# Graph network of four layers on one core: node tables moved with four neighbouring rows per partition

## The chip, the cores and the metric

One core of a Trainium2 chip runs the whole kernel as one launch; the other cores are idle. The metric is the device time of one execution in microseconds, as the median over runs. The kernel before took 3378.82 us (median of 3 runs, 3373.29 to 3382.97).

## The reference, cut to what matters

There are 10,000 nodes with 512 float32 features and 5,000 edges sorted by destination. Each of four layers takes `h = relu(layernorm(x))`, computes something per edge from the source rows of `h`, sums it over the edges of each destination, and adds a node term:

```
h = maximum(layernorm(x), 0)
x = x + L0(h)   # MLP on [h[src], edge_attr], mean over dst, MLP on [h, mean]
x = x + L1(h)   # 8-head attention over edges, sum over dst, + h, layernorm
x = x + L2(h)   # degree-normalised convolution, self loops, relu
x = x + L3(h)   # project to 128, weight, sum over dst, project back to 512
```

About 4 of 10 nodes have an incoming edge; the others get zero for the sum over edges.

## The kernel before, in words

The program runs ten stages one after the other (`program`, L2507). All engines meet between two stages. Each tile in on-chip memory carries the letter of its stage:

- `a` (`prepare`, L138): loads and splits weights, and builds from `src` and `dst` the out-degree of every node, whether it has an incoming edge, and its slot (the row of the edge table that holds its sum). The counts come from one-hot matrices and matrix products: `hl` holds for every edge the partition of its node and the tile of its node.
- `b`, `d`, `f`, `h` (edge stages): gather rows of the node table by `src`, work on 128 edges at a time and write one row of sums per edge to an edge table T in HBM. `s` and `e` are the softmax and the sums of layer 1.
- `c`, `n`, `g`, `i` (node stages, L724, L1499, L1858, L2425): go over the nodes in order. A group is 512 nodes (4 tiles of 128), 20 groups in all. For each group they load the dense rows of the node table from HBM (1 MB), gather the sums from T with four indirect DMAs (one per tile, by `slot`; a node without an edge has an index out of bounds, and its row isn't fetched), compute, and store the dense rows of the next node table (1 MB).

The node tables between stages (`x1`, `x2`, `x3`) are in HBM with one node per row and 10,240 rows; `x2` has 516 columns (2,064 bytes a row), the others 512 (2,048 bytes). Input and output have 10,000 rows. The edge stages gather from these tables by node number.

`group_rows` (L43) is the view through which dense loads and stores see a table: tile j of a group holds rows 128 j to 128 j + 127 of it, one per partition, so each partition takes four rows that lie 256 KB apart. The degree, presence and slot tables (`dis`, `dis2`, `dish`, `has`, `slot`) are [128 partitions x 80 tiles] and follow the same order.

The dense transfers are issued by SyncE in all four node stages, and the final stores by ScalarE's queue; the gathers by GpSimd. In stage `i` the work of a group is: SyncE waits until the store of two groups ago has landed in HBM (L2448), then loads `X` (L2449); ScalarE fills `G` with a constant (L2469), GpSimd gathers over it (L2463); VectorE waits for both and adds them (L2499); ScalarE's queue stores the result (L2477). There are two buffers (b = 0, 1), so the second group runs beside the first. The last group has only 272 nodes, and is loaded and stored tile by tile: 128, 128 and 16 rows (L766, L2482).

Of the kernel before, what the change touches and what calls it, by code (L numbers as in the profile page):

```python
# [6 lines left out]
I32 = mybir.dt.int32  # L7
U32 = mybir.dt.uint32
U16 = mybir.dt.uint16
ALU = mybir.AluOpType  # L10
ACT = mybir.ActivationFunctionType

P = 128
NODES = 10000
# [12 lines left out]
GROUP = 4  # L27
NEW = P - 1
ET = 40
# [3 lines left out]
NG = NT // GROUP  # L33
NR = NG // 2
# [2 lines left out]
EPS = 1e-5  # L37
XW = F + 4
FAR = 1.0e6
assert ET * NEW >= EDGES and NT * P >= NODES and (ET - 1) * NEW < EDGES  # L40


def group_rows(table, g, cols):  # L43

    return table[bass.ds(g * (GROUP * P), GROUP * P), 0:cols].rearrange("(j p) f -> p j f", p=P)


def tiles(x, width=F):
# [37 lines left out]
class Core:  # L86
# [18 lines left out]
    def sb(self, stack, name, shape, dt=F32):  # L105
        return stack.enter_context(self.nc.sbuf_tensor(name, shape, dt))
# [31 lines left out]
def prepare(nc, core, a, keep, l0):  # L138
# [14 lines left out]
    with ExitStack() as st:  # L153
        sb = lambda n, s, d=F32: core.sb(st, "a_" + n, s, d)
        dst_i, nxt_i, src_i, typ_i = (sb(n, [P, ET], I32) for n in ("dst", "nxt", "src", "typ"))
        wgt = sb("wgt", [P, ET])
        emb = sb("emb", [P, HEADS * HEADS])
        hl = sb("hl", [P, 4, ET], I32)
        last = sb("last", [P, ET])
        val = sb("val", [P, ET])  # L160
        iota_i = sb("iotai", [P, P], I32)
# [32 lines left out]
        with nc.Block() as block:  # L194
# [76 lines left out]
            def _(dve):  # L271
                n = 0

                def step(ins):
                    nonlocal n
                    n += 1
                    ins.then_inc(dve_step, 1)
                    dve.wait_ge(dve_step, n)
# [7 lines left out]
                dve.wait_ge(idx_loaded, 16 * 6)  # L286
                step(dve.tensor_copy(iota_f[:, :], iota_i[:, :]))
                for k, ids in enumerate((src_i, dst_i)):
                    step(dve.tensor_scalar(hl[:, 2 * k, :], ids[:, :], 127, None, ALU.bitwise_and))
                    step(dve.tensor_scalar(hl[:, 2 * k + 1, :], ids[:, :], 7, None, ALU.logical_shift_right))  # L290

                step(dve.tensor_tensor(last[:, :], dst_i[:, :], nxt_i[:, :], ALU.not_equal))
                step(dve.tensor_tensor(val[:, :], last[:, :], slot_i[:, :], ALU.mult))
# [430 lines left out]
def layer0_nodes(nc, core, a, keep, T0, x1):  # L724
# [3 lines left out]
    x_loaded = [sem("c_x0"), sem("c_x1")]  # L728
# [7 lines left out]
    stored = [sem("c_st0"), sem("c_st1")]  # L736
# [3 lines left out]
    with ExitStack() as st:  # L740
        sb = lambda n, s, d=F32: core.sb(st, "c_" + n, s, d)
        X = sb("X", [P, 2, GROUP, F])
# [17 lines left out]
        with nc.Block() as block:  # L760
            @block.sync
            def _(sp):
                def load(g, b):
                    sp.dma_start(X[:, b, :, :], group_rows(a["x"], g, F)).then_inc(x_loaded[b], 16)

                def load_last(buf, b, sems):  # L766

                    at = (NG - 1) * GROUP * P
                    left = NODES - at
                    for j in range((left + P - 1) // P):  # L770
                        n = min(P, left - j * P)
                        sp.dma_start(buf[0:n, b, j, :], a["x"][at + j * P:at + j * P + n, :]).then_inc(sems[b], 16)

                def residual(g, b):
                    sp.dma_start(XB[:, b, :, :], group_rows(a["x"], g, F)).then_inc(res_loaded[b], 16)

                def store(r, g, b):
                    sp.wait_ge(o_out, r * GT + (4 * b + 4 + 2))
                    sp.dma_start(group_rows(x1, g, F), XB[:, b, :, :]).then_inc(stored[b], 16)

                for b in range(2):
                    load(b, b)
                sp.dma_start(W3raw, a["L0_gnn_W3"][0:F, :].rearrange("(k p) n -> p k n", p=P)).then_inc(w3_loaded, 16)
                sp.dma_start(W4raw, a["L0_gnn_W4"].rearrange("(k p) n -> p k n", p=P)).then_inc(w_loaded, 16)
                sp.dma_start(b3[:, :], a["L0_gnn_b3"].rearrange("(k p) -> p k", p=P),
                             allow_slow_non_contiguous=True).then_inc(w_loaded, 16)
                sp.dma_start(b4[:, :], a["L0_gnn_b4"].rearrange("(o n) -> o n", o=1).broadcast_to([P, F])).then_inc(w_loaded, 16)
                sp.wait_ge(init, 2)
                with sp.Fori(0, NR - 2) as r:
                    sp.wait_ge(tp_ready, r * TPR + 2 * KF)  # L790
                    for b in range(2):
                        load(r * 2 + (2 + b), b)
                    for b in range(2):
                        sp.wait_ge(stored[b], r * 16)
                        residual(r * 2 + b, b)
                    for b in range(2):
                        store(r, r * 2 + b, b)
                for r in (NR - 2, NR - 1):
                    sp.wait_ge(tp_ready, r * TPR + 2 * KF)
                    for b in range(2):  # L800
                        if r == NR - 1:
                            load(b, b)
                        elif b:
                            load_last(X, b, x_loaded)
                        else:
                            load(2 * r + 2, b)
                    for b in range(2):
                        sp.wait_ge(stored[b], 16 * r)
                        if r == NR - 1 and b:
                            load_last(XB, b, res_loaded)  # L810
                        else:
                            residual(2 * r + b, b)
                    for b in range(2):
                        store(r, 2 * r + b, b)
                for b in range(2):
                    sp.wait_ge(stored[b], 16 * NR)
                    sp.wait_ge(x_loaded[b], 16 * (NR + 1) + 32 * b)

            @block.gpsimd
            def _(pool):  # L820
                pool.memset(G[:, :, :, :], 0.0).then_inc(init, 1)
                pool.memset(XB[:, 1, :, :], 0.0).then_inc(init, 1)
                pool.wait_ge(w_loaded, 48)
                pool.wait_ge(init, 2)

                def round_(r, late):
                    pool.tensor_copy(idx[:, :], keep["slot"][:, bass.ds(r * GT, GT)]).then_inc(idx_staged, 1)
                    pool.wait_ge(idx_staged, r + 1)
                    pool.wait_ge(u_out, r * (2 * GT) + 4)
                    pool.sem_inc(go, 1)  # L830
                    for i in range(GT):
                        pool.indirect_dma_start(G[:, i // GROUP, i % GROUP, :], None, T0[:, :],
                                                bass.IndirectOffsetOnAxis(idx[:, i:i + 1], 0),
                                                bounds_check=ROWS_E - 1, oob_is_err=False).then_inc(run_loaded[i // GROUP], 16)
                    for b in range(2):
                        pool.wait_ge(res_loaded[b], r * 16 + (16 + late * b))
                        pool.tensor_tensor(XB[:, b, :, :], XB[:, b, :, :], over(b4[:, :].unsqueeze(1), [P, GROUP, F]),  # L837
                                           ALU.add).then_inc(res_ready, 1)
                    for b in range(2):
                        pool.wait_ge(run_loaded[b], r * 64 + 64)  # L840
                    pool.sem_inc(go, 1)

                with pool.Fori(0, NR - 1) as r:
                    round_(r, 0)
                round_(NR - 1, 32)

            @block.scalar
            def _(act):
# [41 lines left out]
            def _(dve):  # L890
# [70 lines left out]
                with dve.Fori(0, NR - 2) as r:  # L961
                    round_(r, 0)
                for r in (NR - 2, NR - 1):
                    round_(r, 32)

            @block.tensor
            def _(pe):
# [1457 lines left out]
def layer3_nodes(nc, core, a, keep, x3, T3, out):  # L2425
# [4 lines left out]
    x_loaded, run_loaded, stored = ([sem(f"i_{n}{b}") for b in range(2)] for n in ("x", "g", "st"))  # L2430
    out_ready = sem("i_out")
    with ExitStack() as st:
        sb = lambda n, s, d=F32: core.sb(st, "i_" + n, s, d)
        X = sb("X", [P, 2, GROUP, F])
# [5 lines left out]
        with nc.Block() as block:  # L2440
# [25 lines left out]
            @block.scalar  # L2466
            def _(act):
                def fill(b):
                    act.copy(G[:, b, :, :], over(const[:, :].unsqueeze(1), [P, GROUP, F])).then_inc(filled, 1)  # L2469

                act.wait_ge(const_out, 1)
                fill(0)
                fill(1)
                with act.Fori(0, NR - 1) as r:
                    for b in range(2):
                        act.wait_ge(out_ready, r * 2 + (b + 1))
                        act.dma_start(group_rows(out, r * 2 + b, F), X[:, b, :, :]).then_inc(stored[b], 16)  # L2477
                        fill(b)
                act.wait_ge(out_ready, NG - 1)
                act.dma_start(group_rows(out, NG - 2, F), X[:, 0, :, :]).then_inc(stored[0], 16)  # L2480
                act.wait_ge(out_ready, NG)
                at = (NG - 1) * GROUP * P  # L2482
                for j in range((NODES - at + P - 1) // P):
                    n = min(P, NODES - at - j * P)
                    act.dma_start(out[at + j * P:at + j * P + n, :], X[0:n, 1, j, :]).then_inc(stored[1], 16)
                act.wait_ge(stored[0], 16 * NR)
                act.wait_ge(stored[1], 16 * (NR - 1) + 48)

            @block.vector
            def _(dve):  # L2490
# [124 lines left out]
```

## Time and profile before

| | |
|---|---|
| median of 3 runs | 3378.82 us |
| span of the profiled execution | 3386.8 us |
| busy: TensorE, weight loads, VectorE, ScalarE, GpSimd | 71%, 61%, 53%, 36%, 30% |
| DMA packets | 189,198, 354.10 MB |
| of them SyncE's queue | 129,536, 239.71 MB |
| GpSimd's gathers | 42,880, 91.15 MB |
| ScalarE's queue | 16,688, 21.99 MB |

The span is the time from the first to the last instruction of one profiled execution on the core. It is 8.0 us over the median of the timed runs; no separate device time of this execution is listed. "DMA share" in the rows is the mean busy share of the 16 DMA engines of the core. A DMA is cut into packets; the rows give their number, their bytes and the time they took, as a share of the time of 16 engines. Queue q1 is SyncE's, q10 ScalarE's, q0 GpSimd's.

### The profile page before, as it was taken

Reading aid. Unit: us, or ns where it says so; the run is one execution under the profiler, and the core shown is the slowest. Engines: PE = TensorE matmul, PEld = TensorE weight load, DVE = VectorE, ACT = ScalarE, POOL = GpSimd, SP = SyncE. Lnnn points to the kernel's source line nnn. Section 1 sums busy time; section 2 is a strip of 40 time slices with the busy share of each in tenths; the row PEclk is TensorE's granted clock in tenths of the full one; section 3 lists DMA queues with packets and bytes.
Section 4 is the critical chain, followed back from the end, with each engine's and each line's share of the span. In section 5 each row is a group of like instructions: output and inputs, shape, how many; then the busy total and the mean of one; then the engine's idle time right before and its main releaser. Section 6 shows DMA issues by size and latency. Waiting matters only on the chain. (4 is left out here: it accounts for less than half of the span.)

```text
span 3386.8 us, 41659 instructions
## 1 busy us (share of the span) xinstructions
PE 2409.5 (71%) x13104; PEld 2063.8 (61%) x13104; DVE 1788.8 (53%) x3382; ACT 1223.3 (36%) x2110; POOL 1006.1 (30%) x839
## 2 busy tenths in 40 slices
PE   6779999999969999999979849200005969966600
PEld 6779888888859888888867736100003557754400
DVE  4523232323334544455446565699974579955522
ACT  2133233333333333233335533333324545534421
POOL 0000000000012332233133313566553067752065
PEclk9889999999979999999979965555555589988855
DMA  5101101010224232422243302343434255543388
GB/s 173 37 14 49 37 32 41 27 41 23 41 90 140 87 100 98 140 95 91 81 137 88 85 15 84 121 152 126 139 114 145 82 175 178 179 148 113 112 286 269
DMA packets 189198, 354.10 MB, mean 105 GB/s; under 512 B 28605, under 2 KB 41917, under 8 KB 189097
## 3 DMA queue, kind: packets, MB, share of 16 engines
q1 hardware_dynamic: 129536, 239.71, 20.4%
q0 software_dynamic: 42880, 91.15, 9.7%
q10 hardware_dynamic: 16688, 21.99, 1.9%
q8 instruction: 61, 1.00, 0.1%
q14 instruction: 33, 0.26, 0.0%
HBM read 279.42 MB, written 128.16 MB: 120 GB/s over the span
## 5 line engine op out<-in xcount | busy, mean ns | idle before, releaser
L1848 PE MATMUL f_s_ps<-f_Yh,f_match 128*128 128x258 f32 x80 | 40.1, 501 | 415.3 <-issue 414.7
L1848 PEld LDWEIGHTS f_s_ps<-f_Yh,f_match 128*128 128x128 f32 x80 | 24.7, 309 | 442.0 <-issue 438.0
L132 PE MATMUL b_y_ps<-W23h,b_Rh 128*128 128x320 f32 x800 | 249.1, 311 | 0.0
L470 POOL DMA_INDIRECT b_X<-in_x,b_idx x48 | 48.4, 1008 | 669.3 <-PE b_tp_ps L659 655.4
L133 PE MATMUL b_y_ps<-W23l,b_Rh 128*128 128x320 f32 x800 | 246.2, 308 | 0.5 <-issue 0.5
L134 PE MATMUL b_y_ps<-W23h,b_Rl 128*128 128x320 f32 x800 | 246.1, 308 | 0.3
L132 PE MATMUL b_hid_ps<-b_hTh,W1h 128*128 128x512 f32 x500 | 202.9, 406 | 13.2 <-issue 13.2
L132 PE MATMUL c_u_ps<-c_W3h,c_hTh 128*128 128x320 f32 x640 | 202.0, 316 | 0.0
L133 PE MATMUL b_hid_ps<-b_hTl,W1h 128*128 128x512 f32 x500 | 201.4, 403 | 0.0
L134 PE MATMUL b_hid_ps<-b_hTh,W1l 128*128 128x512 f32 x500 | 201.1, 402 | 0.0
L591 DVE TENSOR_TENSOR b_Rl<-b_R,b_Rh 128x512 fp32r<-128x512 f32 x100 | 69.3, 693 | 248.6 <-ACT b_Rh L524 248.6
L134 PE MATMUL c_u_ps<-c_W3h,c_hTl 128*128 128x320 f32 x640 | 198.4, 310 | 0.0
L133 PE MATMUL c_u_ps<-c_W3l,c_hTh 128*128 128x320 f32 x640 | 198.3, 310 | 0.0
L837 POOL TENSOR_TENSOR c_XB<-c_XB,c_b 128x2048 f32<-128x2048 f32 x20 | 91.6, 4598 | 345.1 <-DMA c_XB<-in_x 345.1
L869 ACT ACTIVATE c_R<-c_tp_ps,c_b 128x512 f32<-128x512 f32 x100 | 68.8, 688 | 323.1 <-PE c_tp_ps L971 314.9
L132 PE MATMUL c_o_ps<-c_W4h,c_zh 128*128 128x512 f32 x400 | 161.8, 405 | 6.4 <-DVE c_zl L917 6.1
L134 PE MATMUL c_o_ps<-c_W4h,c_zl 128*128 128x512 f32 x400 | 156.5, 391 | 0.0
L133 PE MATMUL c_o_ps<-c_W4l,c_zh 128*128 128x512 f32 x400 | 156.1, 390 | 0.0
L616 DVE TENSOR_TENSOR b_Yl<-b_y_ps,b_Yh 128x320 fp32r<-128x320 f32 x80 | 39.4, 492 | 219.9 <-ACT b_Yh L536 219.9
L133 PEld LDWEIGHTS b_y_ps<-W23l,b_Rh 128*128 128x128 f32 x800 | 150.1, 188 | 1.5 <-issue 1.1
L132 PEld LDWEIGHTS b_y_ps<-W23h,b_Rh 128*128 128x128 f32 x800 | 150.0, 188 | 1.1 <-issue 0.7
L134 PEld LDWEIGHTS b_y_ps<-W23h,b_Rl 128*128 128x128 f32 x800 | 149.9, 187 | 0.0
(326 smaller groups left out, 7505.5 us busy)
## 6 DMA issues: line engine op xcount, KB each, us to landing
c_X<-in_x SPq DMA_DIRECT2D x21, 1024.0 KB
x<-n_O SPq DMA_DIRECT2D x20, 1032.0 KB, 4.7
g_X<-x SPq DMA_DIRECT2D x20, 1032.0 KB
x<-c_XB SPq DMA_DIRECT2D x20, 1024.0 KB, 4.7
n_X<-x SPq DMA_DIRECT2D x20, 1024.0 KB, 8.9
x<-g_O SPq DMA_DIRECT2D x20, 1024.0 KB
i_X<-x SPq DMA_DIRECT2D x20, 1024.0 KB
c_XB<-in_x SPq DMA_DIRECT2D x19, 1024.0 KB
```

Source lines behind the costliest of these rows:

```text
L132: pe.matmul(out, ah, bh, start=first, stop=False)
L133: pe.matmul(out, ah, bl, start=False, stop=False)
L134: return pe.matmul(out, al, bh, start=False, stop=last)
L470: pool.indirect_dma_start(X[:, i // GROUP, i % GROUP, :], None, a["x"][:, :], bass.IndirectOffsetOnAxis(idx[:, i:i + 1], 0), bounds_check= ...
L591: dve.tensor_tensor(Rl[:, m, :], R[:, :], Rh[:, m, :].bitcast(F32), ALU.subtract).then_inc(hid_lo, 1)
L616: dve.tensor_tensor(Yl[:, t % 2, w], y[:, h, 0:HALF], Yh[:, t % 2, w].bitcast(F32), ALU.subtract).then_inc(y_out[h], 1)
L837: pool.tensor_tensor(XB[:, b, :, :], XB[:, b, :, :], over(b4[:, :].unsqueeze(1), [P, GROUP, F]), ALU.add).then_inc(res_ready, 1)
L869: act.activation(R[:, k % 2, :], tp[:, k % 2, :], ACT.Relu, bias=b3[:, c:c + 1]).then_inc(z_hi, 1)
L1848: pe.matmul(s[:, 2 * j + h, 0:HW], match[:, b, j, :], Yh[:, j, w], start=True, stop=False)
```

## The change

`group_rows` is turned: partition p holds rows 4 p to 4 p + 3 of the group, so that a partition's four rows are neighbours in HBM. A partition's share of a group is then 8,192 bytes in one piece (8,256 in `x2`) on both sides. The tables follow: a node's partition is bits 2 to 8 of its number, and its tile is four times the bits from 9 up plus the lowest two. The last group covers 68 partitions with all four rows each, moved as 64 and 4 partitions (`LAST`). The edge stages and the tables in HBM stay as they are.

```
+LAST = ((0, 64), (64, 4))
 def group_rows(table, g, cols):
-    return table[bass.ds(g * (GROUP * P), GROUP * P), 0:cols].rearrange("(j p) f -> p j f", p=P)
+    return table[bass.ds(g * (GROUP * P), GROUP * P), 0:cols].rearrange("(p j) f -> p j f", p=P)
@@ prepare: VectorE, for src and dst each
-  step(dve.tensor_scalar(hl[:, 2 * k, :], ids[:, :], 127, None, ALU.bitwise_and))
-  step(dve.tensor_scalar(hl[:, 2 * k + 1, :], ids[:, :], 7, None, ALU.logical_shift_right))
+  step(dve.tensor_scalar(hl[:, 2 * k, :], ids[:, :], 2, 127, ALU.logical_shift_right, ALU.bitwise_and))
+  step(dve.tensor_scalar(within[:, :], ids[:, :], GROUP - 1, None, ALU.bitwise_and))
+  step(dve.tensor_scalar(hl[:, 2 * k + 1, :], ids[:, :], 9, 2, ALU.logical_shift_right, ALU.logical_shift_left))
+  step(dve.tensor_tensor(hl[:, 2 * k + 1, :], hl[:, 2 * k + 1, :], within[:, :], ALU.add))
@@ stage c, SyncE (and the waits on these semaphores: 16 per DMA, so 16 where 32 was)
 def load_last(buf, b, sems):
-    at = (NG - 1) * GROUP * P
-    left = NODES - at
-    for j in range((left + P - 1) // P):
-        n = min(P, left - j * P)
-        sp.dma_start(buf[0:n, b, j, :], a["x"][at + j * P:at + j * P + n, :]).then_inc(sems[b], 16)
+    for p, n in LAST:
+        at = (NG - 1) * GROUP * P + p * GROUP
+        sp.dma_start(buf[p:p + n, b, :, :], a["x"][at:at + n * GROUP, :].rearrange("(p j) f -> p j f", p=n)
+                     ).then_inc(sems[b], 16)
@@ stage i, ScalarE's queue: the store of the last group
-  for j in range((NODES - at + P - 1) // P):
-      n = min(P, NODES - at - j * P)
-      act.dma_start(out[at + j * P:at + j * P + n, :], X[0:n, 1, j, :]).then_inc(stored[1], 16)
+  for p, n in LAST:
+      at = (NG - 1) * GROUP * P + p * GROUP
+      act.dma_start(out[at:at + n * GROUP, :].rearrange("(p j) f -> p j f", p=n), X[p:p + n, 1, :, :]).then_inc(stored[1], 16)
```

## Rows read from the trace of the kernel before

**Rows 1.** Busy time by stretch: stages c, n, g, i (us, engines, clock, DMA, GB/s).

```profile
core 0: us, PE busy (x) PEld busy (x) DVE busy (x) ACT busy (x) POOL busy (x), PEclk, DMA share, GB/s
987.00:1700.00 713.00, 654.41 (x3872) 587.18 (x3872) 356.67 (x628) 239.40 (x389) 186.13 (x115) 0.97 0.32 108
2145.00:2528.00 383.00, 0.00 (x0) 0.00 (x0) 338.74 (x611) 121.22 (x181) 234.62 (x111) 0.50 0.40 133
2707.00:3019.00 312.00, 261.48 (x1280) 213.40 (x1280) 255.08 (x501) 154.19 (x261) 200.16 (x181) 0.94 0.50 166
3196.00:3387.00 191.00, 2.07 (x2) 0.50 (x2) 46.78 (x22) 37.87 (x20) 107.94 (x100) 0.50 0.79 262
```

**Rows 2.** Waits in stage i, 3195 to 3387: us in total, times, longest.

```profile
DVE i_X L2499 <- DMA i_G<-T,i_idx: 93.8, 15, 9.6
DVE i_X L2499 <- DMA i_X<-x: 37.6, 5, 8.9
...
SPq L2449 <- DMA out<-i_X: 146.3, 16, 22.8
```

**Rows 3.** Chain that ended last, one turn of stage i: start, us, what.

```profile
3269.76 8.63 DMA out<-i_X
...
3278.55 8.14 DMA i_X<-x
```

**Rows 4.** DMA from 327.2 to 331 us: one 256 KB load, one 320 KB store.

```profile
DMA packets 288, 0.59 MB, mean 155 GB/s; under 512 B 32, under 2 KB 32, under 8 KB 288
```

**Rows 5.** DMA from 3204 to 3206 us: only node rows, 2,048-byte packets.

```profile
DMA packets 411, 0.81 MB, mean 406 GB/s; under 512 B 15, under 2 KB 15, under 8 KB 411
q1 hardware_dynamic: 411, 0.81, 106.1%
```

**Rows 6.** DMA from 41 to 43 us: only a weight, 5,120-byte packets.

```profile
q1 hardware_dynamic: 163, 0.83, 102.6%
```

**Rows 7.** DMA queues from 3208 to 3387 us: packets, MB, share of 16 engines.

```profile
q1 hardware_dynamic: 9504, 18.88, 33.8%
q10 hardware_dynamic: 10352, 20.48, 31.5%
q0 software_dynamic: 6400, 8.10, 14.2%
```

**Rows 8.** Waits for loads, gathers and stores in stages c, n, g.

```profile
DVE n_G L1641 <- DMA n_G<-T,n_idx: 20.7, 5, 6.6
...
DVE n_raw L1620 <- DMA n_X<-x: 14.9, 1, 14.9
...
DVE c_raw L897 <- DMA c_X<-in_x: 9.5, 2, 9.3
...
SPq L1925 <- DMA x<-g_O: 3.9, 1, 3.9
```

**Rows 9.** Start of the kernel, VectorE: start, us, instruction, idle before.

```profile
11.66 0.18 DVE L289 TENSOR_SCALAR a_hl<-a_src 128x40 int32<-128x40 int32 x1
...
14.80 0.83 DVE L282 CAST rows<-a_rows 128x1280 uint16<-128x1280 int32 x1 [1.83 <-DMA a_rows<-in_dst_row]
```

**Rows 10.** End of the kernel: last add and the three last stores.

```profile
3380.57 2.29 DVE L2499 TENSOR_TENSOR i_X<-i_X,i_G 128x2048 f32<-128x2048 f32 x1 [1.14 <-DMA i_G<-T,i_idx]
3382.90 1.35 ACTq L2485 DMA_DIRECT2D out<-i_X  x3
```

**Rows 11.** Stage n: the last gather of a round and who waited for it.

```profile
2303.54 1.21 POOL L1565 DMA_INDIRECT n_G<-T,n_idx  x1 [0.30 <-issue]
...
2310.26 5.65 DVE L1641 SCALAR_TENSOR_TENSOR n_G<-n_G,has,n_H 128x512 f32<-128x512 f32 x2 [6.38 <-DMA n_G<-T,n_idx]
```

**Rows 12.** DMA queues from 2305.5 to 2308.5 us, the whole list.

```profile
q1 hardware_dynamic: 404, 0.83, 98.0%
```

**Rows 13.** Stage i, gathers and fills: busy us, mean ns | idle.

```profile
L2463 POOL DMA_INDIRECT i_G<-T,i_idx x80 | 99.9, 1248 | 72.3 <-ACT i_G L2469 51.3 <-issue 16.4 <-POOL i_idx L2458 2.7
...
L2469 ACT COPY i_G<-i_const 128x2048 f32<-128x2048 f32 x20 | 37.9, 1898 | 145.2 <-DVE i_X L2499 127.4 <-DVE i_const L2494 17.8
```

More of the change, by code:

```diff
@@ L39 @@
 FAR = 1.0e6
+LAST = ((0, 64), (64, 4))
+assert (NG - 1) * GROUP * P + sum(n for _, n in LAST) * GROUP == NODES and len(LAST) == 2
 assert ET * NEW >= EDGES and NT * P >= NODES and (ET - 1) * NEW < EDGES
 def group_rows(table, g, cols):
-    return table[bass.ds(g * (GROUP * P), GROUP * P), 0:cols].rearrange("(j p) f -> p j f", p=P)
+    return table[bass.ds(g * (GROUP * P), GROUP * P), 0:cols].rearrange("(p j) f -> p j f", p=P)
 def tiles(x, width=F):
@@ L158, in prepare @@
         hl = sb("hl", [P, 4, ET], I32)
+        within = sb("within", [P, ET], I32)
         last = sb("last", [P, ET])
@@ L816, in _ @@
                     sp.wait_ge(stored[b], 16 * NR)
-                    sp.wait_ge(x_loaded[b], 16 * (NR + 1) + 32 * b)
+                    sp.wait_ge(x_loaded[b], 16 * (NR + 1) + 16 * b)
             @block.gpsimd
@@ L844, in _ @@
                     round_(r, 0)
-                round_(NR - 1, 32)
+                round_(NR - 1, 16)
             @block.scalar
@@ L963, in _ @@
                 for r in (NR - 2, NR - 1):
-                    round_(r, 32)
+                    round_(r, 16)
             @block.tensor
@@ L2481, in _ @@
                 act.wait_ge(out_ready, NG)
-                at = (NG - 1) * GROUP * P
-                for j in range((NODES - at + P - 1) // P):
-                    n = min(P, NODES - at - j * P)
-                    act.dma_start(out[at + j * P:at + j * P + n, :], X[0:n, 1, j, :]).then_inc(stored[1], 16)
+                for p, n in LAST:
+                    at = (NG - 1) * GROUP * P + p * GROUP
+                    act.dma_start(out[at:at + n * GROUP, :].rearrange("(p j) f -> p j f", p=n), X[p:p + n, 1, :, :]).then_inc(stored[1], 16)
                 act.wait_ge(stored[0], 16 * NR)
-                act.wait_ge(stored[1], 16 * (NR - 1) + 48)
+                act.wait_ge(stored[1], 16 * (NR - 1) + 32)
             @block.vector
```

## The prediction

> **What bounds the kernel now.** I read the busy time by stage first [rows 1]. In stage c TensorE works 92% of the time and the DMA engines 32%; stage g is TensorE, VectorE and GpSimd with DMA at 50%; stage n is VectorE (339 of 383 us). Only the last stage, i, is bound by transfers: VectorE works 47 of 191 us and the DMA engines are busy 79% of the time. Next I read who waits there [rows 2]: VectorE's adds wait 93.8 us for the gathers (15 times of 20) and 37.6 us for the dense load (5 times), and SyncE waits 146.3 us for stores to land before it may load into the same buffer. The chain of waits shows the loop [rows 3]: a store of 1 MB takes 8.6 us from its issue to its landing, the load that follows it 8.1 us. With the add (2.3 us [rows 10]) and the issues this is a turn of some 19 us for two groups. So a change in what 1 MB costs the DMA engines is felt in stage i, and at the other node stages only where they start, end, or wait for a gather.
>
> **Does the change make larger packets at all?** It does if four neighbouring rows become one packet. The edge attributes are loaded in just such a shape, [128 partitions, 4, 128] contiguous on both sides. In that stretch there are 288 packets: 128 of 2,560 bytes and 16 small ones of the store, which leaves 144 for the 256 KB load, that is 128 pieces of 2,048 bytes and 16 small ones [rows 4]. Unmerged there would be 512 pieces. So I expect 128 packets of 8,192 bytes for each MB where there are 512 now.
>
> **What a packet costs.** Undisturbed, 396 packets of 2,048 bytes (411 less the 15 small) took 106.1% of 16 engines in 2 us: 33.95 us / 396 = 85.7 ns [rows 5]. Packets of 5,120 bytes took 102.6% x 32 us / 163 = 201.4 ns [rows 6]. The line through both is 8.6 ns a packet plus 0.0377 ns a byte, so 8,192 bytes would take 317 ns against 4 x 85.7 = 343 now. A MB is 8 such packets on each engine: 8 x 26 ns = 0.21 us less, of some 2.7. The bounds are 0 (both rates are near one ceiling, 406 and 0.83 MB / 2 us = 415 GB/s) and what follows.
>
> In stage i packets cost more than that: SyncE's take 33.8% x 179 us x 16 / 9,216 = 105 ns (18 loads of 512), ScalarE's 31.5% x 2,864 us / 10,000 = 90 ns [rows 7]. Over the undisturbed 85.7 this is 9,216 x 19.3 / 16 + 10,000 x 4.5 / 16 = 11.1 + 2.8 = 13.9 us per engine. If this excess is paid per packet, three quarters of it go (10.4 us); if per byte, nothing. No row says which. I take a fifth of that, 2 us, since packets two and a half times larger show none of it changing beyond the line, and keep 0 and 10.4 for the range.
>
> On small pieces the Trainium skill (DMA: Bandwidth & Descriptors, Why small descriptors are slow) gives about 3 cycles of fixed overhead a packet, at the 850 MHz of its fabric 3.5 ns; my fit of this trace has 8.6. By that page the saving would be, as an estimate, 24 packets x 3.5 ns = 0.08 us a MB, and the last stage would gain about 3 us instead of 8. The measured line decides here.
>
> **The sum, part by part.**
> Stage i: 39 dense MB (20 loads, 19 full stores) x 0.21 = 8.2 us, plus 2 for the excess. Adds wait for gathers more often than for loads, but a gather itself lands only after the dense transfer ahead of it has drained: the last gather of a round in stage n was issued at 2303.5 and waited for until 2310.3, and for three of those microseconds the list of queues shows SyncE's alone, at 98% [rows 11, 12]. So dense transfers are in both chains. The engines are busy 79% of the stage; that share of 10.2 us is -8.1 us. If the dense time were never what ends last, it would be 0.
> Starts: VectorE waits for the first 1 and 2 MB in c and n [rows 8], and g opens like c: 4 x 0.21 = -0.8. Ends: SyncE waits 3.9 us for a last store in each of c, n and g (one row stands for three): -0.6.
> Stage n waits 20.7 us for gathers in 5 rounds of 10 [rows 8]; with the longest at 6.6 that is about three full waits, each behind two dense MB: 3 x 2 x 0.21 = -1.3, of which I take half, -0.6, bounds 0 and -1.3. Other dense transfers of c, n and g are loaded ahead and hidden by TensorE or VectorE; if this cover were gone, they would gain too, not lose.
> Stage a: four more small VectorE steps (0.18 us, 0.22 with the gap: 0.9 us). The conversion behind them waits 1.83 us for its own load [rows 9], so they are hidden: 0; uncovered, +0.9.
> Last group: in c two loads and residuals lose one issue on SyncE's queue, none of which is waited for: 0. At the end of i, three stores at 1.35 us of issue become two [rows 10]: -0.45. The one that carries the data now has 64 partitions. No row shows a 64-partition store; the three stores and their landing take 3.9 us from issue to the end (3382.9 to 3386.8), so I bound the effect by -0.5 and +1.2 (its 0.5 MB at half of 415 GB/s is 2.5 us against 1.3) and take +0.4, together 0.
> The Trainium skill (SBUF, State Buffer, Door 1: The DMA port swizzle) speaks against this one: partitions 0 to 63 reach only half of the 16 ports. By it the last store would run at half rate, an estimate of 1.2 us more; no trace here shows it.
>
> Sum: -8.1 - 0.8 - 0.6 - 0.6 = -10.1 us. The profiled span would go from 3386.8 to 3376.7; it is 8.0 us over the median, so the median goes from 3378.8 to 3368.7. I forecast **3369 us**.
>
> **The rivals.**
> A. The excess goes with the packets, and all of it is exposed: stage i gains (8.2 + 10.4) x 0.79 to x 1.0 = 15 to 19 us, with the 2 us elsewhere 17 to 21: 3358 to 3362, 3360 in the middle. For it: loads cost 105 ns a packet beside stores and 86 alone. Against: what disturbs them may be the memory, which sees the same bytes.
> B. The gain is hidden. GpSimd spends 4 x 1.25 us on a group's gathers, and add, fill and gather form a loop of their own (2.3 + 0.5 + 1.9 + 5.0 us and the landing of some 4) [rows 13]. If that loop sets the pace, only starts and ends are left, -1 to -3: 3376 to 3378. Against: a turn is 19 us now, this loop some 14.
> C. The other side: the gathers are held back longer. A gather is in small pieces: 6,400 packets in 80 gathers, 5 for each engine [rows 7]. If a piece must let one dense packet pass, it waits 317 ns where it waited 86: 5 x 0.23 = 1.2 us for a gather that shares the engines. The last gather of a group decides in 15 of 20 adds [rows 2]: +18 us, and +3 to +6 in n's rounds, against the -10.1 above: +11 to +14, 3390 to 3393. It decides from about 0.55 us a gather on, in more than half of the groups. For it: 15 of 20. Against: in rows 12 the queues don't take turns; the gather waits for the whole transfer, and that gets shorter. The Trainium skill (DMA: Bandwidth & Descriptors, Queues, rings and completion order) has the engines go round the queues packet by packet, which would make C the rule.
> D. The view isn't merged, or merged only on one side: 512 packets stay, 3378 to 3380. Against: rows 4.
>
> **How the numbers follow.** Forecast (own range -5 to -15, 3364 to 3374): 0.50. A: 0.17. B and D: 0.20 (0.17 and 0.03). C: 0.13, of which a third ends near zero. A difference of 0.3% is 10.1 us, about what this kernel's runs tell from nothing (they spread by 9.7 us). My forecast stands on that line, so half of its chance is on either side: faster 0.25 + 0.17 = 0.42; same 0.25 + 0.20 + 0.04 = 0.49; slower 0.09. The range reaches from A's far end with the spread of the runs, 3352, to the middle of C, 3386.
>
> **What would show it.** Right: SyncE's packets fall from 129,536 by 160 x 384 = 61,400 (c moves 60 full MB on it, n and g 40 each, i 20) and ScalarE's by 7,300; 8 KB packets at some 317 ns; stage i shorter by 6 to 10 us and no other stage by more than 2; store and load of the chain nearer 8.2 and 7.8 us. A: stage i shorter by over 14. B: the turn unchanged with adds waiting for gathers 20 of 20. C: waits for gathers in i and n longer than 93.8 and 20.7 us. The prediction is wrong if stage i gets longer, or if a stage that I call covered moves by over 3 us.

## The result, and the profile after

The changed kernel takes 3351.52 us (median of 5 runs, 3344.72 to 3364.01) against 3378.82 before (5 runs, 3373.29 to 3383.71). The medians are 27 us apart; the ratio of the runs is 0.9929, 95% interval 0.9907 to 0.9952, or 24 us. I had forecast 3369, a gain of 10. The direction is right and the size is not: the gain is 2.4 to 2.7 times the forecast, and the time lies half a microsecond below the low end of my range (3352).

The profiled span went from 3386.8 to 3358.2 us. By stage, in us from the first instruction of one to the first of the next (b is 828.1 and 826.3, s and e together 184.5 and 184.3):

| | a | c | d | n | f | g | h | i |
|---|---|---|---|---|---|---|---|---|
| before | 159.4 | 711.6 | 261.4 | 383.2 | 179.4 | 312.3 | 176.5 | 190.4 |
| after | 160.2 | 689.9 | 258.7 | 386.8 | 179.0 | 310.5 | 176.2 | 186.3 |

Stage c, which I had called covered, gave 21.7 us; stage i, on which the forecast stood, gave 4.1 instead of 8.1. The windows of c and i of the kernel after answer to [rows 1]: VectorE's busy time in c fell by 13.3 us with the same 628 instructions, so some of them had been slower before.

```profile
core 0: us, PE busy (x) PEld busy (x) DVE busy (x) ACT busy (x) POOL busy (x), PEclk, DMA share, GB/s
986.50:1676.40 689.90, 652.33 (x3872) 586.95 (x3872) 343.38 (x628) 239.61 (x389) 188.15 (x113) 0.97 0.30 112
...
3171.90:3358.20 186.30, 2.08 (x2) 0.50 (x2) 46.77 (x22) 37.89 (x20) 111.23 (x100) 0.50 0.76 269
```

**The packets.** The page after lists SyncE's queue (q1) with 61,904 packets fewer than before for the same bytes, and ScalarE's (q10) with 7,528 fewer:

```profile
q1 hardware_dynamic: 67632, 239.71, 19.2%
q0 software_dynamic: 42880, 91.15, 9.7%
q10 hardware_dynamic: 9160, 21.99, 1.8%
```

What an 8 KB packet costs undisturbed stands in the list of queues of the kernel after from 2127 to 2132 us, the answer to [rows 5]. Less 32 small ones there are 259 in q1's line: 100.4% x 5 us x 16 / 259 = 310 ns, against 343 for four of 2 KB and my 317.

```profile
DMA packets 296, 2.13 MB, mean 426 GB/s; under 512 B 32, under 2 KB 32, under 8 KB 37
...
q1 hardware_dynamic: 291, 2.12, 100.4%
```

**Stage i.** The queues from 3185 to 3358 us (173 us; before, [rows 7], it was 179):

```profile
q1 hardware_dynamic: 2592, 18.88, 32.2%
q10 hardware_dynamic: 2824, 20.48, 29.8%
q0 software_dynamic: 6334, 8.02, 15.1%
```

A full packet of q1 takes 32.2% x 173 x 16 / 2,304 = 387 ns where four took 420. That is 77 ns over the undisturbed 310; before it was 420 - 343 = 77 as well. ScalarE's stores went from 361 to 330 ns per 8 KB, 18 and 20 ns over. In this stage none of the excess went with the packets. The two queues together are busy for 62.0% x 173 = 107.3 us where it was 65.3% x 179 = 116.9: 9.6 us less, against 10.2 in my sum.

The waits of stage i after, to set beside [rows 2], show that loads hardly end last any more:

```profile
DVE i_X L2502 <- DMA i_G<-T,i_idx: 118.9, 18, 9.6
DVE i_X L2502 <- DMA i_X<-x: 7.7, 2, 4.2
```

Gathers and loads together held the adds for 131.4 us before (93.8 and 37.6) and 126.6 now. The chain of waits, which went through a store and a load at [rows 3], now goes mostly through the add, ScalarE's fill and the gather; here is one of its turns, in the columns of [rows 3]:

```profile
3318.49 1.91 ACT i_G L2473
...
3323.88 2.22 POOL i_G L2467
3326.40 6.63 DMA i_G<-T,i_idx
3333.12 2.30 DVE i_X L2502
```

**The end.** The last add and the last stores after (compare [rows 10]), and the queue of those stores from 3350 to 3358.2 us. From the first issue to the end it is 3352.5 to 3358.2 = 5.7 us, where it was 3.9; I had forecast no difference.

```profile
3350.14 2.29 DVE L2502 TENSOR_TENSOR i_X<-i_X,i_G 128x2048 f32<-128x2048 f32 x1 [8.26 <-DMA i_G<-T,i_idx]
3352.47 1.31 ACTq L2488 DMA_DIRECT2D out<-i_X  x2
```

```profile
q10 hardware_dynamic: 88, 0.56, 32.2%
```

32.2% x 8.2 us x 16 / 68 full packets is 621 ns each, twice the undisturbed 310. The last stores of the kernel before, mostly from 128 partitions, stand in its list of queues from 3382.9 to 3386.8 us. Less 64 small ones there are 316 packets of 2 KB at 94 ns, or 377 ns per 8 KB:

```profile
q10 hardware_dynamic: 380, 0.65, 47.7%
```

The Trainium skill (SBUF, State Buffer, Door 1: The DMA port swizzle) has partitions 0 to 63 reach half of the ports. The trace agrees in part: 8 KB on each of 16 engines in 621 ns is 211 GB/s, half of the 423 of undisturbed loads, but the last stores before ran at 348 only.

**Stage c, where the gain is.** The rows of VectorE's operation `c_zl = c_R - c_zh`, first before, then after (busy us, mean ns of one | idle):

```profile
L917 DVE TENSOR_TENSOR c_zl<-c_R,c_zh 128x512 fp32r<-128x512 f32 x100 | 100.2, 1025 | 63.5 <-ACT c_zh L870 35.9 <-issue 16.7 <-ACT c_R L869 10.8
```

```profile
L921 DVE TENSOR_TENSOR c_zl<-c_R,c_zh 128x512 fp32r<-128x512 f32 x100 | 86.6, 889 | 55.0 <-ACT c_zh L874 29.1 <-ACT c_R L873 13.8 <-issue 12.1
```

The list of `c_zl` gives 676 ns as its shortest and 4,806 as its longest before, and 677 and 3,764 after. One round of c (two groups) shows what holds it. In the rows of before, GpSimd adds the bias to the residual once that has landed, and a `c_zl` that starts inside these 9.13 us ends only with them:

```profile
1085.10 1.80 SPq L764 DMA_DIRECT2D c_X<-in_x  x2
...
1098.72 9.13 POOL L837 TENSOR_TENSOR c_XB<-c_XB,c_b 128x2048 f32<-128x2048 f32 x2 [36.62 <-DMA c_XB<-in_x]
...
1103.60 5.41 DVE L917 TENSOR_TENSOR c_zl<-c_R,c_zh 128x512 fp32r<-128x512 f32 x2 [0.64 <-ACT c_zh L870]
```

The same three rows after:

```profile
1083.23 1.68 SPq L769 DMA_DIRECT2D c_X<-in_x  x2
...
1094.78 9.20 POOL L841 TENSOR_TENSOR c_XB<-c_XB,c_b 128x2048 f32<-128x2048 f32 x2 [33.93 <-DMA c_XB<-in_x]
...
1101.77 3.37 DVE L921 TENSOR_TENSOR c_zl<-c_R,c_zh 128x512 fp32r<-128x512 f32 x2 [0.63 <-ACT c_zh L874]
```

From the first load's issue to the add it was 13.6 us and is 11.6: the residual lands 2.1 us earlier. So the adds begin 7.0 us ahead of VectorE instead of 4.9, and what is left of them when `c_zl` comes is 2.2 us instead of 4.2. The two operations (1.4 us alone) took 5.4 and take 3.4.

The other rounds are alike: in each of the ten, before and after, one `c_zl` meets the adds and ends 0.55 us behind them. Its time fell by 1.6 to 2.0 us in the first eight rounds and not at all in the last two. Together this is the 13.6 us of the two rows above. TensorE's transposes wait for the split. These are the waits of PE for `c_zl`, before:

```profile
PE c_tp_ps L971: 21.5, 20
PE c_o_ps L132: 6.1, 5
```

And after, 18.6 us less, near the stage's 21.7:

```profile
PE c_tp_ps L975: 7.6, 12
PE c_o_ps L134: 1.4, 2
```

That is the theory that the experiments test: **larger packets let the residual land earlier, and GpSimd's add gets out of the way of VectorE's split.** Why 2.1 us, when my line gives 5 MB x 0.21 = 1.0? The queue list of the 20 us from the first of these loads on (before: 1085 to 1105, after: 1083.2 to 1103.2) has

```profile
GB/s 352 389 389 332 242 176 156 184 319 356 348 373 410 336 393 418 381 397 402 406 406 393 385 385 385 389 389 385 389 180 29 12 0 0 0 0 0 0 0 0
DMA packets 2640, 5.24 MB, mean 262 GB/s; under 512 B 80, under 2 KB 80, under 8 KB 2640
...
q1 hardware_dynamic: 2640, 5.24, 75.4%
```

before and

```profile
GB/s 360 508 295 508 131 131 377 410 442 393 426 442 377 475 442 360 459 410 426 459 393 459 459 360 442 328 49 0 0 0 0 0 0 0 0 0 0 0 0 0
DMA packets 710, 5.16 MB, mean 258 GB/s; under 512 B 80, under 2 KB 80, under 8 KB 80
...
q1 hardware_dynamic: 710, 5.16, 64.5%
```

after. Less 80 small packets, 8 KB cost 4 x 75.4% x 320 us / 2,560 = 377 ns before and 64.5% x 320 / 630 = 328 after, 49 ns less instead of 26. A slow stretch behind the store is part of it: four half microseconds at 156 to 242 GB/s before, two at 131 after. Here, unlike in stage i, half of the excess (34 to 18 ns) went with the packets. 5 MB x 8 packets x 49 ns is 2.0 us, which is the 2.1.

### The profile page after: what moved, and what is told of

It is laid out like the page before. It is cut to its first block and busy times, and to the rows that moved or that the text cites. A ratio compares the mean times of both kernels' runs of the same rounds, so it can differ in the third digit from the quotient of the medians.

```text
span 3358.2 us, 41660 instructions
## 1 busy us (share of the span) xinstructions
PE 2403.5 (72%) x13104; PEld 2060.3 (61%) x13104; DVE 1775.6 (53%) x3386; ACT 1224.0 (36%) x2110; POOL 1001.8 (30%) x839
## 5 line engine op out<-in xcount | busy, mean ns | idle before, releaser
L475 POOL DMA_INDIRECT b_X<-in_x,b_idx x48 | 48.4, 1008 | 668.1 <-PE b_tp_ps L664 654.2
```

The source lines that it names most:

```text
L475: pool.indirect_dma_start(X[:, i // GROUP, i % GROUP, :], None, a["x"][:, :], bass.IndirectOffsetOnAxis(idx[:, i:i + 1], 0), bounds_check= ...
```

## The experiments

Each is compared with the kernel before on its own chip. Stage times are from one profile each, in us, by the starts of the stages as above; `c_zl` is its mean in ns.

| kernel | ratio to before, 95% interval | c | `c_zl` | n | i |
|---|---|---|---|---|---|
| after | 0.9929 [0.9907, 0.9952] | 689.9 | 889 | 386.8 | 186.3 |
| e1_small_packets | 0.9972 [0.9952, 0.9993] | 702.2 | 1010 | 376.5 | 195.6 |
| e11_small_packets_again | 0.9984 [0.9969, 0.9999] | 702.7 | 1006 | 376.8 | 192.9 |
| e2_small_in_c | 0.9951 [0.9926, 0.9976] | 700.9 | 1008 | 372.7 | 187.0 |
| e3_before_residual_first | 0.9954 [0.9934, 0.9974] | 693.0 | 691 | 367.5 | 189.2 |
| e4_after_residual_first | 0.9937 [0.9912, 0.9962] | 690.4 | 691 | 378.4 | 188.4 |
| e5_before_no_add | 0.9939 [0.9923, 0.9954] | 680.6 | 690 | 375.9 | 190.0 |
| e6_after_no_add | 0.9888 [0.9872, 0.9903] | 679.8 | 690 | 371.7 | 185.2 |
| e9_after_again | 0.9897 [0.9883, 0.9911] | 685.8 | 896 | 371.6 | 180.9 |
| e10_before_again | 0.9998 [0.9988, 1.0009] | 702.7 | 1012 | 377.1 | 189.1 |
| e12_after_adds_in_pieces | 0.9898 [0.9870, 0.9925] | 683.7 | 801 | 373.1 | 184.4 |
| e13_before_adds_in_pieces | 0.9905 [0.9879, 0.9932] | 686.6 | 892 | 372.0 | 192.4 |
| e14_after_pieces_residual_first | 0.9941 [0.9916, 0.9967] | 690.4 | 690 | 382.6 | 188.0 |

e5, e6, e9 and e10 ran on another chip, where the kernel before takes 3302 us; stages d, f and h are shorter there for both kernels, so only ratios and the stages c, n and i are compared across chips.

**Packets of 2 KB in the new order.** Four spare elements behind each row keep the tile from being one piece; e1 has it in c, n, g and i, e2 in c alone, e11 is e1 again.

```
-X = sb("X", [P, 2, GROUP, F])
+X = sb("X", [P, 2, GROUP, F + 4])[:, :, :, 0:F]
```

> The changed kernel, with the tiles of all dense loads and stores given a row pitch of 4 elements more, so that a partition's four rows are neighbours in HBM but not on chip: the order of rows and all tables stay as changed, and each MB is cut into 512 packets of 2 KB again. Theory 1 (the gain comes from larger packets): the gain is gone, 3374 to 3384 us, stage c back from 690 to about 712 us, the packets of SyncE's queue back at about 129,500. Theory 2 (the gain comes from the order in which the memory is walked, four neighbouring rows per partition): the gain stays, 3347 to 3360 us, stage c about 690 us.

> The changed kernel with the wider row pitch in stage c alone (X and the residual tile), so 2 KB packets there and 8 KB packets in n, g and i. Theory 1 (most of the gain lies in stage c, where the residual lands earlier and GpSimd's add of the bias meets VectorE's split of the hidden rows for a shorter time): stage c about 712 us, the split of zl at about 1,025 ns mean, the whole 20 to 23 us slower than the changed kernel, 3370 to 3376 us. Theory 2 (stage c's 22 us are a matter of this one execution, and the gain lies in n, g, i): within 4 us of the changed kernel, 3348 to 3358 us.

> The changed kernel with its new row order, but with four spare elements behind each 512-element row of the X and XB tiles of stage c, the X and O tiles of stages n and g and the X tile of stage i, so that the merged transfers move in 2,048-byte packets. Theory packet size (the gain comes from fewer, larger packets, by way of earlier landings): the ratio to the kernel before is about 1.000 (0.997 to 1.002), stage c takes about 702 us and stage i 189 to 190 us. Rival row order (neighbouring rows per partition help whatever the packet size): ratio 0.990 to 0.995, stage c 686 to 690 us.

With the small packets stage c is back at 700.9 to 702.7 us and `c_zl` at 1,006 to 1,010 ns: the new row order doesn't do it, the packets do, and e2 shows it with the packets of c alone (the 11 us are of its profile; its ratio stands only 7 us from that of the changed kernel, where I expected 20 to 23). Stage i goes to 195.6 and 192.9. What e1 and e11 keep of the gain, 0.16% to 0.28%, is 5 to 9 us that neither theory had; whether it is the row order, the wider pitch or scatter was not settled.

**The residual loaded ahead of the activations**, so that the add is over before VectorE's split begins.

```
+for b in range(2):                     # stored[b], then residual(2 * r + b, b) or load_last
+    ...
 sp.wait_ge(tp_ready, r * TPR + 2 * KF)
 for b in range(2):
     load(r * 2 + (2 + b), b)
 ...
-for b in range(2):                     # the residual, from behind the loads
-    ...
```

> The kernel before with one thing moved: in stage c SyncE issues the two residual loads of a round ahead of the two loads of the next rows, not behind them. Packets stay at 2 KB. Collision theory: the residual lands about 5 us earlier, GpSimd's adds end before VectorE's split begins, the split falls from a mean of 1,025 ns to about 690 to 750 ns, stage c from 712 to 680 to 690 us, the whole 3347 to 3360 us: as much as the change gains or more, without any larger packet. Rival (larger packets help TensorE's stage in some other way, for example by less traffic beside its reads): stage c stays within 4 us of 712.

> The changed kernel with the same move: residual loads ahead of the loads of the next rows. Collision theory: what is left of the collision goes too (the split's mean of about 890 ns to 690 to 750), stage c from 690 to 678 to 686 us, the whole 3338 to 3348 us, faster than both kernels; and between this kernel and the one before with the same move only stages n, g, i and the ends are left, 3 to 8 us. Rival: the rows now come later, and VectorE's statistics wait for them: stage c 5 us or more longer than 690.

In e3 the split is at its undisturbed 691 ns with packets of 2 KB, and stage c loses 10 to 19 us to the two profiles of before (702.7 and 711.6). One round of e3, to set beside the rows of before: the add runs from 1096.4 to 1105.7, and the first split begins behind it.

```profile
1096.44 9.24 POOL L837 TENSOR_TENSOR c_XB<-c_XB,c_b 128x2048 f32<-128x2048 f32 x2 [29.52 <-DMA c_XB<-in_x]
...
1108.02 0.69 DVE L917 TENSOR_TENSOR c_zl<-c_R,c_zh 128x512 fp32r<-128x512 f32 x1 [0.63 <-ACT c_zh L870]
```

With this collision gone for both, the packets are worth 2.6 us in c (693.0 and 690.4), not 20. But both stages are longer than expected (680 to 690 and 678 to 686), and e4 gains nothing on the changed kernel (0.9937 and 0.9929), though its `c_zl` is 200 ns shorter a piece. The reason stands at the start of the stage. The first adds now run while VectorE splits the weights W4 (`c_W4l`), again with two operands in on-chip memory, and that is held instead. The row of the kernel after, then two of e4:

```profile
1019.75 2.83 DVE L128 TENSOR_TENSOR c_W4l<-c_U,c_W4h 128x2560 fp32r<-128x2560 f32 x1 [1.54 <-ACT c_W4h L123]
```

```profile
1015.16 9.14 POOL L841 TENSOR_TENSOR c_XB<-c_XB,c_b 128x2048 f32<-128x2048 f32 x2
...
1017.03 9.96 DVE L128 TENSOR_TENSOR c_W4l<-c_U,c_W4h 128x2560 fp32r<-128x2560 f32 x1 [1.53 <-ACT c_W4h L123]
```

So 7.1 us are lost once, and the first `c_zl` comes 58.9 us after the start of the stage instead of 50.5. The time from the first `c_zl` of a round to that of the next is 64.6 us in e4 and 65.3 in the kernel after, so the later rounds win back most of it. VectorE waits no longer for the activations than before the move (8.3 us against 8.6), so the rival that I had named isn't the reason.

**No add**, in c only: four columns in place of 512. The output of this layer then lacks the bias in the other 508 columns.

```
-pool.tensor_tensor(XB[:, b, :, :], XB[:, b, :, :], over(b4[:, :].unsqueeze(1), [P, GROUP, F]),
+pool.tensor_tensor(XB[:, b, :, 0:4], XB[:, b, :, 0:4], over(b4[:, 0:4].unsqueeze(1), [P, GROUP, 4]),
```

> The kernel before with the collision taken away where it starts: in stage c GpSimd adds the bias b4 to 4 columns of the residual only, not to all 512, so the other 508 columns of the layer's output lack b4 (left out). Loads, waits and packets stay. Collision theory: without the two adds of 4.6 us a round, VectorE's split of zl takes 690 ns each time, stage c goes from 712 to 685 to 695 us. Rival (early transfers help the stage by themselves): stage c stays above 702 us.

> The changed kernel with the same part left out (b4 is added to 4 of 512 columns). Collision theory: it has nothing more to gain in stage c, 685 to 692 us, within 3 us of the kernel before without the add: the size of the packets then makes no difference to this stage. Rival (larger packets help stage c beyond the collision): 8 us or more shorter in stage c than the kernel before without the add.

> The changed kernel, unedited, once more, to have its stages a second time and its time beside the same runs of the kernel before as the experiments. If the stage times of the first look are the kernel's own: c 687 to 693 us, i 185 to 188, n 367 to 387 (this stage has moved by 19 us between executions whatever the packets), the ratio to before 0.991 to 0.995. If stage c's 690 us was chance: c over 698.

> The kernel before, unedited, for a second profile. If its stage c is its own: 708 to 715 us with the split of zl at a mean of 1,000 to 1,040 ns. If the residual's arrival moves the collision from execution to execution: c anywhere from 695 to 712, and the 22 us of the first pair of profiles overstate the change; the stage's mean gain is then 10 to 15 us.

This is the sharpest test. Both stages are even shorter than expected. Without GpSimd's add stage c takes 680.6 us with 2 KB packets and 679.8 with 8 KB ones. So of the 16.9 us that the same two kernels differ by in c on this chip with the add (702.7 and 685.8), 16 need the add. The second profiles also show that the first pair's 21.7 us in c overstates the change by some microseconds: the kernel before has 711.6 in one and 702.7 in the other, on another chip. Stage i of e9, 180.9 us, is outside the 185 to 188 expected. e9 and e10 repeat the result there: 0.9897 against 0.9998, a gain of 33 us (from 3302) with c 16.9, i 8.2 and n 5.5 of it. e5 and e6 still differ by 0.51%, 17 us, of which their profiles show 12.4 (3271.0 and 3258.6), 0.8 in c.

**The adds of c and n in four pieces**, meant to leave gaps in which VectorE gets its turn; in e14 with the residual first as well.

```
+for j in range(GROUP):
+    add = pool.tensor_tensor(XB[:, b, j, :], XB[:, b, j, :], b4[:, :], ALU.add)
+add.then_inc(res_ready, 1)
```

> The changed kernel, with GpSimd's bias adds of stage c and stage n made as four instructions of 128x512 in place of one of 128x2048. Theory collision (VectorE's operations on two SBUF operands stand still while one long GpSimd add runs): no such VectorE operation is held for more than about a quarter of 4.6 us, stage c takes 680 to 685 us and stage n 345 to 365 us, the whole 20 to 30 us less than the changed kernel. Rival (the two engines share the port element by element, or the lock is for the sum of the adds): stage c stays at 684 to 690 us, stage n at 370 to 387 us.

> The kernel before with the same adds in pieces. Theory collision: most of what the change gains in stage c is the escape from the collision, so stage c is within 3 us of the changed kernel's with pieces, and the two kernels with pieces differ by 8 to 12 us, what stage i and the ends are worth. Rival: the difference stays at 27 to 36 us.

> The changed kernel with adds in pieces and with the residual of stage c loaded ahead of the activations. Theory collision: with pieces the place of the add no longer matters, so it is within 3 us of the kernel with pieces alone. Rival (the order still matters, since an add in front of the splits never meets them and one behind does): stage c shorter by 5 us or more than with pieces alone, or longer by as much if the activations' later landing costs more.

No `c_zl` takes over 1,782 ns now. In e13 this alone (in c and n), with the old packets, gives c 686.6 us and a ratio of 0.9905: about as much as the whole change. GpSimd's adds in c end later for it (109.4 us of work instead of 91.6), so it isn't their end or what GpSimd does behind them that made the stage long, but what they hold up. Stage c differs from e12's by 2.9 us, as the theory wanted. The totals of e12 and e13 are 0.9898 and 0.9905, 2 us apart where I expected 8 to 12; the intervals are each about 9 us to either side, so this neither confirms nor refutes it, and their profiles have i 8.0 us apart. Stage n was a miss: 373 us, not 345 to 365. The operation on `n_G`, which the long add had held, is quicker, and the time comes back as waiting for gathers. Stage n of the kernel after, and of e12:

```profile
L1645 DVE SCALAR_TENSOR_TENSOR n_G<-n_G,has,n_H 128x512 f32<-128x512 f32 x80 | 133.3, 1676 | 27.8 <-DMA n_G<-T,n_idx 24.2 <-ACT n_H L85 3.7
```

```profile
L1647 DVE SCALAR_TENSOR_TENSOR n_G<-n_G,has,n_H 128x512 f32<-128x512 f32 x80 | 84.5, 1066 | 59.4 <-DMA n_G<-T,n_idx 59.4
```

48.8 us less busy, 31.6 more idle, and GpSimd's own adds cost 125.2 us in pieces against 96.3. e14 is no better than e12, and its profile has c 6.7 us longer, so the order still matters. It is `c_W4l` again, and here the pieces don't help: it comes in the third of eight pieces and ends 2.7 us behind the last, after 9.46 us.

```profile
1016.63 9.98 POOL L842 TENSOR_TENSOR c_XB<-c_XB,c_b 128x512 f32<-128x512 f32 x8
...
1019.84 9.46 DVE L128 TENSOR_TENSOR c_W4l<-c_U,c_W4h 128x2560 fp32r<-128x2560 f32 x1 [1.54 <-ACT c_W4h L123]
```

Why `c_zl` gets in between two pieces and `c_W4l` doesn't is open. The best time is e12's, 3341.63 us, 10 us less than the changed kernel by the ratios where I expected 20 to 30, but its interval overlaps that of the changed kernel, so it is shown to be faster only than the kernel before.

## Why the prediction was right or wrong

**Larger packets: right.** 61,904 and 7,528 packets fewer, against 61,400 and 7,300. Rival D is out.

**The cost of a packet: nearly right.** 310 ns undisturbed, against 317: 33 ns less than four small ones instead of 26.

**The excess of stage i: too high.** I gave a fifth of it to the packets; none went (77 ns per 8 KB before and after). The two errors cancel: 9.6 us of DMA time, against 10.2. Rival A, whose extra came from this excess, is nearest in its total (3358 to 3362), but by accident: it wanted stage i over 14 us shorter.

**Stage i, -8.1: not settled.** It got 4.1 us shorter in the first pair of profiles and 8.2 in the second. The profiles with 8 KB packets in i (after, e2, e4, e6, e9, e12, e14) have it at 185.7 us on average (180.9 to 188.4), those of the old order (before, e3, e5, e10, e13) at 190.2, and the new order with 2 KB (e1, e11) at 194.3. By these means the packets are worth 8.5 us, near my term, and everything else that changed costs 4.0, of which 1.8 is the last store. With such a spread that is an indication only, and the padded pitch of e1 and e11 may be part of it, in which case the packets are worth less. Rival B, that the loop of add, fill and gather takes over, is half true: gathers end 18 of 20 waits, in e9 all 20, as B wanted, but the stage still got shorter.

**The last store, 0: wrong.** It costs 1.8 us. The 64 packets, four for each engine, take 4 x 621 ns = 2.5 us, as the estimate at half the rate had it: that is the +1.2 of my upper bound, of which I had taken 0.4. The issue saved nothing against it: two take 1.31 us and three took 1.35. By the packets of e10 and e9 the stores took 1.7 us from the first packet to the end of the last and take 3.3, and the first packet starts 0.35 us later behind the first issue; that is all of the 1.8.

**Starts and ends, -1.4, and n's gathers, -0.6: the right way, too small for the total.** The waits for the first loads of c, n and g fell by 2.9 us together in the first pair and 1.6 in the second (forecast 0.8), those for their last stores by 1.0 (forecast 0.6). The waits of n for gathers went from 20.7 to 24.2 us and in the second pair from 15.3 to 10.5. Stage n itself is anywhere between 367.5 and 386.8 us in fourteen profiles, whatever the packets. The four steps in a: a is 0.8 us longer in the first pair and 0.9 in the second, so they may not have been hidden as I said, but a spreads from 157.9 to 160.2 over all profiles.

**Rival C: wrong.** The adds of i wait for gathers and loads together 4.8 us less (8.9 in the second pair, 130.7 to 121.8), and the stage got shorter. The sign that I had named for C, waits for gathers alone longer than 93.8 us, came true (118.9) and proves nothing; what rose was only who came last.

**The step that failed** is "other dense transfers of c, n and g are loaded ahead and hidden by TensorE or VectorE; if this cover were gone, they would gain too, not lose". In c that is false, and by my own measure (a covered stage moves by over 3 us) the prediction is wrong there. TensorE and VectorE didn't wait for the residual's landing, only GpSimd did, whose idle time I took for harmless. But it starts an add that holds VectorE's split for as long as it runs, so an earlier landing moved work of 9 us out of VectorE's way by 1.6 to 2.0 us in each of the first eight rounds. The term stood at nothing, and it was the largest. That the total still came out at the edge of my range is luck: that end of the range was Rival A's, and A is wrong.

Stage c is where it shows. The mean of c over the profiles with the add in one piece and the activations first is 707.2 us before (711.6, 702.7) and 687.9 after (689.9, 685.8), 19.3 us; without the add 0.8, with the add in pieces 2.9, with the residual first 2.6. One thing stays open: the stage gains more than the hold loses. Against the same kernel without the add, e9, whose 100 `c_zl` take 20.6 us more than in e6, has a c 6.0 us longer, but e10, with 32.2 us more than in e5, one 22.1 us longer. The last 12 us of hold cost 16, and the runs don't show why. The rows were there: a `c_zl` of 5.41 us beside others at 0.69, under a GpSimd row of 9.13.

As a check on the total, weight the differences of the ratios by their intervals: the pairs with the collision taken away (e3 and e4, e5 and e6, e12 and e13) differ by 6, 17 and 2 us, together about 12, near the 10 of my sum; the pairs with it (before and after, e10 and e9) by 24 and 33, together about 30. The 18 between the two are about what stage c shows. The 17 of e5 and e6 say that the packets may be worth a little more elsewhere than the profiles can tell.

## What to carry to other kernels

When a transfer gets faster, follow what its landing starts, also where nobody on the critical path waits for it: an operation that starts at once on GpSimd can move into or out of the way of VectorE. Look for this in a trace by the longest time of a small VectorE operation against its shortest (here 4.81 us and 0.68), and what ran on GpSimd at that moment. Then test it by shortening or splitting the other engine's operation, which here (e13) gave about as much as the whole change of layout. Moving the operation instead can let it meet another one, as it met `c_W4l` in e3, e4 and e14.

## What the runs showed of the hardware

- A `c_zl` (VectorE, two operands in on-chip memory) that meets GpSimd's add doesn't slow down in proportion, it stands still until the add ends: 5.41 us for two beside 1.4 alone, and in all ten rounds, before and after, the one that is held ends 0.55 us behind the adds, wherever it began; 0.69 us each once the add is gone. The Trainium skill (SBUF, State Buffer, Who interferes with whom) calls the port pair that the two engines share an exclusive lock and has a VectorE instruction with two SBUF inputs contend with a GpSimd instruction that reads SBUF; the traces agree. With pieces of 1.4 us on average no split takes over 1.8 us (e12, e13).
- The hold need not end with one instruction: `c_W4l` (128x2560) took 9.96 us instead of 2.83 across two adds (e4) and 9.46 across what was left of eight pieces (e14).
- It doesn't always pay to split the long add: in n the 96.3 us of adds became 125.2, and the stage (373.1 us) stayed within its scatter.
- A last store of mostly 64 partitions took 621 ns per 8 KB packet; the last stores before, of 128 partitions, 377 ns per 8 KB; undisturbed loads 310.
- Behind a store a load starts slowly (131 to 242 GB/s in half microseconds, against 320 to 475 later), for about 2 us with 2 KB packets and 1 us with 8 KB ones, in the one round of c looked at.
